# Value products and value sums over blocks of two heads in place of four

## The reference

```
qh = q.reshape(B, S, 16, 16)                       # k, v: both ctx
scores = einsum('bsqd,bskd->bsqk', qh, kh) / 4
scores = where(tril(ones((16, 16))), scores, -1e18)  # head q sees heads 0..q
attn = softmax(scores, -1)
out = einsum('bsqk,bskd->bsqd', attn, vh)
```

## Time and profile before

| | |
|---|---|
| median of 3 runs | 1121.16 us (1119.32 to 1122.7) |
| the profiled execution, its own time | 1123.83 us |
| its span | 1122.0 us |
| PE busy | 982.4 us, 88% |
| DVE busy | 955.9 us, 85% (2185 instructions) |
| POOL busy | 903.8 us, 81% (862 instructions) |
| ACT busy | 863.6 us, 77% |
| value products (line 349) | 256 instructions on POOL, 384.3 us |
| value sums (line 1644) | 256 instructions on DVE, 192.1 us |

### The profile page before, as it was taken

How to read it: one execution, slowest core, us unless ns; L and a number is a source line. 1 busy time by engine, 2 the same in 40 slices (tenths; PEclk the granted TensorE clock), 3 DMA queues, 4 the chain that set the end, 5 groups by cost and what they waited for, 6 DMA issues and landing times.

```text
span 1122.0 us, 15669 instructions
## 1 busy us (share of the span) xinstructions
PE 982.4 (88%) x4160; PEld 614.9 (55%) x4160; DVE 955.9 (85%) x2185; ACT 863.6 (77%) x1585; POOL 903.8 (81%) x862
## 2 busy tenths in 40 slices
PE   2689698999999999999999999999999999879505
PEld 1337274656657474756566574757565564646303
DVE  3854999999999999999999999999999899667561
ACT  3766779889797979798897979797897979464603
POOL 0221999989898989989898989899898989878880
PEclk9889899999999999999999999999999999889756
DMA  6120010111101111111111011111111100111001
GB/s 195 38 57 1 19 38 1 38 39 39 38 20 20 57 20 38 37 38 38 37 38 31 26 19 56 19 38 38 38 39 38 18 22 19 19 38 20 19 0 39
DMA packets 38317, 38.72 MB, mean 35 GB/s; under 512 B 2660, under 2 KB 37864, under 8 KB 38248
## 3 DMA queue, kind: packets, MB, share of 16 engines
q1 hardware_dynamic: 29800, 29.58, 8.3%
q0 software_dynamic: 8448, 8.39, 4.9%
HBM read 29.58 MB, written 8.39 MB: 34 GB/s over the span
## 4 chain that ended last, share of the span: by engine, by line
ACT 25%; POOL 25%; DVE 20%; issue 17%; PE 9%; SPq 1%; DMA 1%; DVEq 0%; POOLq 0%; ACTq 0%
POOL prod L349 18%; DVE psum L1644 7%; ACT n L482 5%; PE psum L893 4%; ACT hidden L617 4%; POOL prod L327 4%; DVE stat L1418 3%; ACT v_dh L586 2%; DVE psum L1585 2%; ACT xr L507 2%; DVE x L1593 2%; ACT rr L544 2%; DVE pp L1516 1%; POOL prob L336 1%; ACT e L540 1%
## 5 line engine op out<-in xcount | busy, mean ns | idle before, releaser
L327 POOL TENSOR_TENSOR prod<-q,kv_ctx 128x256 f32<-128x256 f32 (+5 forms) x448 | 360.0, 847 | 65.5 <-ACT q L482 65.5
L349 POOL TENSOR_TENSOR prod<-prob,v_dh 128x256 f32<-128x256 f32 (+3 forms) x256 | 384.3, 1705 | 17.5 <-ACT prob L592 17.5
L893 PE MATMUL psum<-xk,w_key 128*128 128x512 f32 x512 | 230.6, 604 | 14.0 <-DVE xk L1481 14.0
L1644 DVE TENSOR_REDUCE psum<-prod 128x64 f32<-128x256 f32 (+3 forms) x256 | 192.1, 819 | 50.1 <-POOL prod L349 49.9
L947 PE MATMUL psum<-w_val,hidden 128*128 128x256 f32 x1024 | 226.3, 379 | 0.0
L947 PEld LDWEIGHTS psum<-w_val,hidden 128*128 128x128 f32 x1024 | 193.5, 190 | 32.6 <-issue 7.6
L1615 DVE TENSOR_REDUCE score<-prod 128x16 f32<-128x256 f32 (+5 forms) x448 | 175.7, 467 | 11.7 <-POOL prod L327 11.7
L893 PEld LDWEIGHTS psum<-xk,w_key 128*128 128x128 f32 x512 | 97.6, 193 | 131.1 <-issue 120.4
L442 ACT ACT_TABLE_LOAD x96 | 123.2, 1283 | 2.6 <-PEq L1803 0.9
L907 PE MATMUL psum<-ident,n 128*128 128x128 f32 x384 | 60.0, 290 | 69.4 <-ACT n L482 58.1
L907 PEld LDWEIGHTS psum<-ident,n 128*128 128x128 f32 x384 | 46.9, 148 | 100.1 <-issue 70.0
(11 more groups left out here) (97 smaller groups left out, 1785.7 us busy)
## 6 DMA issues: line engine op xcount, KB each, us to landing
x_in<-in_x SPq DMA_DIRECT2D x16, 512.0 KB, 3.5
kv_ctx<-in_ctx SPq DMA_DIRECT2D x16, 512.0 KB, 4.5
x<-in_x POOLq DMA_DIRECT2D x16, 512.0 KB, 5.8
out<-x SPq DMA_DIRECT2D x16, 512.0 KB, 3.2
w_key<-in_wkey SPq DMA_DIRECT2D x1, 1024.0 KB
w_val<-in_wval SPq DMA_DIRECT2D x1, 1024.0 KB
w_v<-in_v SPq DMA_DIRECT2D x2, 256.0 KB
w_k<-in_wk SPq DMA_DIRECT2D x1, 256.0 KB, 3.6
```

Of the source, the lines that this page charges most:

```text
L327: ins = pool.tensor_tensor(o, a, b, ALU.mult)
L349: ins = pool.tensor_tensor(o, ph[:, HB * n:HB * n + HB, 0:keys].unsqueeze(2).to_broadcast(shape), vh[:, :, 0:keys].unsqueeze(1).to_broadca ...
L893: mm = pe.matmul(to[:, :], w[:, fi, P * f:P * f + P], src[:, fi, :], start=(fi == 0), stop=(fi == CH - 1))
L1644: ins = dve.tensor_reduce(bank[SUM_BANK][:, row:row + HB * HD], src, AX.X, ALU.add)
```

## The change

The value side gets its own block height, `VB = 2`, while the scores keep `HB = 4`. The eight blocks of a tile have 2, 4, 6, ... 16 keys, so its products have 64, 128, 192, ... 512 elements a partition, 2304 in all. There are eight products on POOL and eight sums on DVE per token tile where there were four of each, and each sum writes 32 elements. The orders of calls, the semaphores and what they wait for are as they were.

```diff
 HB = 4
 NB = NH // HB
+VB = 2
 
 def value_parts():
     parts, at = [], 0
-    for i in range(NB):
-        keys = HB * (i + 1)
+    for i in range(NH // VB):
+        keys = VB * (i + 1)
         parts.append((i, keys, at))
-        at += HB * HD * keys
+        at += VB * HD * keys
     return parts, at
 
 # value_products
                 for n, keys, at in V_PARTS:
-                    shape = [P, HB, HD, keys]
-                    o = prod[slot][:, at:at + HB * HD * keys].rearrange("p (a d b) -> p a d b", a=HB, d=HD)
+                    shape = [P, VB, HD, keys]
+                    o = prod[slot][:, at:at + VB * HD * keys].rearrange("p (a d b) -> p a d b", a=VB, d=HD)
                     ins = pool.tensor_tensor(
-                        o, ph[:, HB * n:HB * n + HB, 0:keys].unsqueeze(2).to_broadcast(shape),
+                        o, ph[:, VB * n:VB * n + VB, 0:keys].unsqueeze(2).to_broadcast(shape),
                         vh[:, :, 0:keys].unsqueeze(1).to_broadcast(shape), ALU.mult)
 
 # sum_values
                 for n, keys, at in V_PARTS:
-                    src = prod[slot][:, at:at + HB * HD * keys].rearrange("p (a b) -> p a b", b=keys)
-                    row = C * (t % 2) + HB * HD * n
-                    ins = dve.tensor_reduce(bank[SUM_BANK][:, row:row + HB * HD], src, AX.X, ALU.add)
+                    src = prod[slot][:, at:at + VB * HD * keys].rearrange("p (a b) -> p a b", b=keys)
+                    row = C * (t % 2) + VB * HD * n
+                    ins = dve.tensor_reduce(bank[SUM_BANK][:, row:row + VB * HD], src, AX.X, ALU.add)
```

## The result

The changed kernel took 1125.26 us (median of 8 runs, 1122.17 to 1128.47) against 1120.68 us before (8 runs, 1119.32 to 1122.7): a ratio of 1.0040, 95% interval 1.0022 to 1.0058. It is slower by 4.6 us, where +4.2 was forecast.

The account below looks back on a forecast made before the run. The prediction took a ring of waits over POOL, DVE and ACT, 61.86 us a pass, as the bound. POOL's +4.6 us and DVE's -0.4 made +4.2, so 1125.4 us; range 1113 to 1136, the forecast's own 1123 to 1128.

Parts of the forecast that it names:

- The ring: Loop pass of 61.86 us: POOL's value products to DVE's sums to ACT's probabilities and back; every piece counts in full.
- E: Rival: DVE already bounds some passes from tile 0 on, so the change does nothing: 1121 to 1122 us; chance 0.10.
- rival C: POOL: the cheap rate belongs to short value products, tile 0.127 us cheaper than now: 1114.3 us; chance 0.18.
- DVE's price: Value sums: four more instructions +0.25 us, 256 fewer elements -0.27: -0.014 a tile, -0.4 us over 29 tiles.
- D: Rival: DVE pays each record in full, 145 ns instead of 63, +0.35 us a tile: 1136 us; chance 0.04.
- POOL's price: Value products on POOL: the changed tile costs +0.09 us more, +4.6 us over 51 tiles.
- the line: POOL product time by size, drawn through score products: 2.13 ns an element up to 256, 2.12 above.
- the overlap: POOL: each product's record overlaps the next, 0.042 us taken off each, 0.34 us for eight.
- the built tile: POOL's changed tile, not in the trace, built from score-product records: eight sizes 6.38 us less 0.34 overlap, 6.04 us.
- A: Rival on POOL: part-filled runs of 6, 10, 14 keys cost a fetch more, +0.165 us a tile: 1133.8 us; chance 0.20.
- The count, 51 tiles: Value-product tiles on the path: three in each of 13 groups, four in each of the last three.
- The sum: Whole kernel: POOL +4.6 and DVE -0.4 give +4.2 us, median from 1121.2 to 1125.4 us.

Follow-up runs that it names:

- the split products and sums: Two runs on the kernel before: POOL's four products each split into two of two heads, 1149.31 us; DVE's four sums each split in two, 1128.11 us.
- the key groups: Kernel before with POOL's four products each taking four keys for all heads from 4c up, written to rows of 16 keys: 1106.5 us, ratio 0.9888.
- the two timed comparisons: Changed kernel against the kernel before, timed twice without further edit: 1125.26 against 1120.68 us, then 1127.62 against 1120.04 us.

## Why the prediction was right, point by point

**What bounds.** The ring over POOL, DVE and ACT was right, and that POOL's tiles 0 to 2 and DVE's tiles 2 and 3 lie on it: the pass grew by 0.35 us where the waits ahead of the sums grew, and the split products and sums moved the time by what their tile prices say. What I had missed is the second ring. The prediction took the chain of one pass for thirteen groups, and in three of the twelve passes the chain of the kernel before leaves POOL behind tile 0 or runs over TensorE. So E was right in kind. It is small: at tile 2's sum the rings tie to within 0.1 us there, and those three passes grew by 0.30, 0.26 and 0.34 us, the others by 0.31 to 0.40. For a faster change it is large: the second ring would have capped rival C at about 0.3 us a pass (61.96 - 61.64).

**DVE's price, -0.014 a tile.** Right to 0.02 us. The sum is 2.98 us in place of 3.01, and eight sums in place of four cost nothing when POOL's price is gone. D is refuted by both. The Trainium skill's advice to keep the number of operations low ("VectorE: DVE Perf Modes", section "Rules for kernel authors") agrees with the trace in sign, at 0.058 us an instruction, but not in the size of D, because the next operation starts before the last one's record ends.

**POOL's price, +0.09 a tile.** This is the mis-sized term: it measured +0.15 (6.035 on average against 5.885), and the tile is just above the 5.93 to 6.02 us that were to show the forecast. The fixed cost, the element rate and the four-key product were as read from the rows. The sizes that no row showed were not on the line: two keys 23 ns below it, six, ten and fourteen 18, 27 and 36 above, +58 ns together. The value products of 8, 12 and 16 keys lie 30 ns below the line of the score products, and the overlap is 0.32 us in place of 0.34. With these three the built tile of 6.04 - 0.05 = 5.99 us comes to the measured one. A was right that part-filled runs cost extra, with 81 ns in place of the 165 I gave it; C was right for two keys only (298 ns, where it had 253 and the overlap of 42).

The Trainium skill's floor, as the prediction uses it, does not hold for the four-key product. In the changed tile 128 elements take 403 ns, 54 below the line, so the saving that the floor denies is there, and the key groups' tile of 4.91 us has it for all 2560 elements. The section that the prediction names gives the floor as about 2.6 cycles, not 2.5, and does not speak of patterns; "whatever the pattern" is my reading.

**The count, 51 tiles.** Right but for tiles 1 and 2 of the three passes above. And a tile behind the DMA's issue passes on less. From the start of tile 2's products to DVE's sum it is 590.07 - 583.65 = 6.42 us before and 591.84 - 585.35 = 6.49 after, +0.07 where the start-to-start price is +0.145. Behind the issue a product's record is longer. For the tile's last product it is 0.44 us before (2797 ns where tile 1's takes 2357), but 0.38 us after (1637 ns against 1262), and this difference makes up nearly all of the missing 0.075. Why the records are longer is not shown. Thus a pass took 2 x 0.15 + 0.07 - 0.03 = +0.34 us in place of 0.24.

**The sum.** From the trace it is 12 passes of 0.34 us, 0.4 in the first group, and some 0.5 to 0.7 in each of the last three: +6 us. The forecast of +4.2 was too small by the POOL term, and the two timed comparisons of +4.6 and +7.6 stand on either side of 6. So the hit on 4.6 is partly luck, the scatter of the clock. The sign and the order of size were earned, the tenths were not.

## What to carry to other kernels

A triangular mask tempts to finer blocks. Weigh the elements saved against one fixed price for every instruction added, engine by engine, and start to start (here 0.14 us on GpSimd and 0.06 on VectorE): 10% fewer elements paid for it on VectorE and not on GpSimd. Look also at the shape that each finer block takes, because the price of an unseen run length is what an estimate gets wrong. Before claiming a gain from shortening a ring of waits, read the chain over several passes and look for the second ring just under it.

## What the runs showed of the hardware

GpSimd's product of two float32 operands cost 2.1 ns an element, but 1.70 where one operand repeats in a group of four elements or stands still (4.92 us in place of 5.885 for 2560 elements). Runs that don't fill a group of four cost extra (6 keys 396 ns, where 4 take 293 and 8 take 450). Cutting by key groups, or reordering the loop and writing with a stride, brings the whole tile to the lower rate. Its writes 4 to 16 elements apart were free, whereas VectorE's reads 16 elements apart cost 1.70 ns in place of 1.04. Why either is so, no run shows. The two kernels built on this, at ratios of 0.9888 and 0.9867, beat both the kernel before and the changed one.
